# Last batch's natural scores: four row strips written in two pairs, each pair behind its own maxima, and no constant matmuls ahead of them

## The reference

```
x = layernorm(x + bitlinear_attention(x))          # block a
q = concat([ctx, x]) @ Wq                          # block b, per batch of 8
k = x @ Wk; v = x @ Wv; ssm_k = ctx @ Wsk; ssm_v = ctx @ Wsv
delta = pos[:, None] - pos[None, :]
mask = (delta >= 0) & (delta < 64)                 # for both streams
scores = einsum('bhqd,bhkd->bhqk', q, kcat) / 4 + alibi
wei = softmax(where(mask, scores, -inf)); o = wei @ vcat
x = layernorm(x + o @ Wo)
x = layernorm(x + x @ base_w.T + base_b + lora_of_top2_experts(x))   # block c
```

## Time and profile before

| | |
|---|---|
| median of 3 runs | 920.82 us (917.58, 920.82, 921.01) |
| the profiled execution | 920.37 us, of which 918.2 us are the span from first to last instruction |
| PE busy | 805.0 us (88%) |
| DVE busy | 515.8 us (56%) |
| ACT busy | 322.8 us (35%) |
| granted PE clock | 0.995 of full speed on average |

### The profile page before, as it was taken

The page is one execution under the profiler, slowest core; times in us unless marked ns, Lnnn a source line. Parts: engine busy times, 40 slices in busy tenths (PEclk is TensorE's granted clock), DMA queues, the critical chain, the costliest instruction groups (busy, mean ns, idle before and its releaser), DMA issues.

```text
span 918.2 us, 22670 instructions
## 1 busy us (share of the span) xinstructions
PE 805.0 (88%) x10223; PEld 518.4 (56%) x10275; DVE 515.8 (56%) x1061; ACT 322.8 (35%) x423; POOL 85.5 (9%) x103
## 2 busy tenths in 40 slices
PE   3888977888999989988899989988898978998996
PEld 2464763467635874467635864567545864474343
DVE  4645386437945487437845486447845383425233
ACT  5252323442243323442244323432244314230422
POOL 1102002000210012000300012000300010010001
PEclk9999999999999999999999999999999999999999
DMA  9512501000001000010001000010001000000000
GB/s 343 181 47 46 72 1 24 25 2 1 11 15 47 2 2 24 1 48 1 25 1 47 2 2 24 1 47 2 1 1 47 3 1 1 24 2 1 1 24 24
DMA packets 18879, 27.08 MB, mean 29 GB/s; under 512 B 5464, under 2 KB 7640, under 8 KB 18784
## 3 DMA queue, kind: packets, MB, share of 16 engines
q1 hardware_dynamic: 18640, 25.61, 9.3%
q10 hardware_dynamic: 144, 0.03, 0.0%
HBM read 21.44 MB, written 4.19 MB: 28 GB/s over the span
## 4 chain that ended last, share of the span: by engine, by line
PE 62%; DVE 19%; ACT 13%; issue 4%; POOL 1%; DMA 1%; ACTq 0%; POOLq 0%; SPq 0%; DVEq 0%
ACT p_b L740 9%; DVE max_b L1457 7%; PE ps L1118 7%; PE ps L1154 6%; PE ps L1039 6%; PE ps L1195 5%; PE ps L1022 4%; PE ps L1083 4%; PE ps L1059 3%; PE ps L870 2%; PE ps L943 2%; PE ps L1127 2%; PE ps L953 2%; PE ps L1047 2%; PE ps L838 2%
## 5 line engine op out<-in xcount | busy, mean ns | idle before, releaser
L740 ACT ACTIVATE p_b<-ps 128x2048 f32<-128x2048 f32 x64 | 106.5, 1664 | 116.1 <-PE ps L1127 116.1
L1457 DVE TENSOR_REDUCE max_b<-ps 128x4 f32<-128x768 f32 (+2 forms) x160 | 106.5, 709 | 39.5 <-PE ps L1097 21.3
L1083 PE MATMUL ps<-k_b,q_b 32*128 32x192 f32 (+2 forms) x1024 | 55.7, 332 | 25.7 <-DVE max_b L1457 23.6
L1118 PE MATMUL ps<-q_b,k_b 32*128 32x512 f32 (+1 forms) x512 | 66.2, 586 | 12.8 <-ACT p_b L740 7.0
L1483 DVE STREAM_TRANSPOSE o_nat<-ps 128x512 f32<-128x512 f32 x32 | 21.0, 695 | 98.2 <-PE ps L1143 98.2
L1083 PEld LDWEIGHTS ps<-k_b,q_b 32*128 32x128 f32 x1024 | 39.2, 184 | 43.1 <-DVE max_b L1457 37.1
L1143 PE MATMUL ps<-p_b,v_b 128*32 128x256 f32 (+1 forms) x1024 | 61.7, 358 | 2.0 <-ACT p_b L740 2.0
L1022 PE MATMUL ps<-c_t,wq 128*128 128x256 f32 x256 | 60.4, 385 | 2.9 <-DVE out_a L1380 1.9
L1337 DVE SCALAR_TENSOR_TENSOR nat<-ps,st_a,qkv_bias 128x512 f32<-128x512 f32 x48 | 35.3, 738 | 48.0 <-PE ps L870 47.7
L1195 PE MATMUL ps<-base_t,x_t 128*128 128x512 f32 x128 | 62.0, 609 | 0.3 <-DVE x L1562 0.3
L1039 PE MATMUL ps<-x_t,wq 128*128 128x256 f32 x256 | 60.0, 384 | 0.2 <-ACT x_t L694 0.2
(11 more groups left out here) (193 smaller groups left out, 1414.2 us busy)
## 6 DMA issues: line engine op xcount, KB each, us to landing
x_in<-x SPq DMA_DIRECT2D x8, 512.0 KB, 3.6
p_b<-ctx SPq DMA_DIRECT2D x8, 512.0 KB, 4.3
y<-x SPq DMA_DIRECT2D x7, 512.0 KB, 3.0
p_b<-L_attn_qkv_w SPq DMA_DIRECT2D x2, 1024.0 KB, 6.6
p_b<-L_xattn_Wq SPq DMA_DIRECT2D x1, 2048.0 KB, 14.8
x<-L_attn_qkv_w SPq DMA_DIRECT2D x2, 512.0 KB, 9.6
x<-L_ffn_base_w SPq DMA_DIRECT2D x2, 512.0 KB, 7.8
wo<-L_xattn_Wo SPq DMA_DIRECT2D x8, 128.0 KB, 7.5
```

Source lines behind the costliest of these rows:

```text
L740: act.activation(p_b[:, j % 2, :, 0:cols], ps[:, 4:8, 0:cols], ACT.Exp, scale=DB ** -0.5).then_inc(pb_here.sem, 1)
L1083: pe.matmul(bank(4 + r)[:, (i % 2) * N:(i % 2) * N + 2 * n * S], q_b[strip[r], i, :, :].rearrange("p h q -> p (h q)"), k_b[strip[r], half, ...
L1118: pe.matmul(bank(4 + r)[:, 0:nb * P], k_b[strip[r], half, 2 * j:2 * j + 2, :, :].rearrange("p c s k -> p (c s k)"), q_b[strip[r], 2 * j:2 ...
L1457: ins = dve.tensor_reduce(max_b[:, half, 0, i:i + k, 2 * n:2 * n + 2], ps[:, 4 + 2 * n:6 + 2 * n, :].rearrange("p r (i n) -> p i r n", i=2 ...
```

## The change

For the last batch alone (`alone`), stage b2 writes strips 0 and 1 first and then strips 2 and 3, each as a group of its own. From pair 1 on, each group waits for one count of `sb_max`: strips 0 and 1 for the maxima of banks 4 and 5 of the pair before, strips 2 and 3 for those of banks 6 and 7. The matmuls of constants ahead of the eight pairs (24 of them) are gone. Every other batch does what it did, and the lists of DVE, ACT, POOL and SP are the same.

```diff
@@ -1064,39 +1064,43 @@
             strip = [slice(r * S, (r + 1) * S) for r in range(4)]
 
             def b2(b, half, pair):
-                keep_on(b, NB - 1, (0, 0, 6, 6, 4, 4, 2, 2)[4 * half + pair])
-                if pair:
+                alone = isinstance(b, int) and b == NB - 1
+                if pair == 0:
+                    if half:
+                        mb_here(pe, b, 1)
+                    else:
+                        q_here(pe, b)
+                        k_here(pe, b)
+                        v_here(pe, b)
+                        if not alone:
+                            ct_here(pe, b + 1)
+                elif not alone:
                     sb_max(pe, b, 8 * half + 2 * pair)
-                elif half:
-                    mb_here(pe, b, 1)
-                else:
-                    q_here(pe, b)
-                    k_here(pe, b)
-                    v_here(pe, b)
-                    if not (isinstance(b, int) and b + 1 >= NB):
-                        ct_here(pe, b + 1)
                 seen = [(i, slice(max(i - 2, 0), i + 1)) for i in (2 * pair, 2 * pair + 1)]
                 o = lambda r, i, n: bank(4 + r)[:, (i % 2) * N:(i % 2) * N + 2 * n * S].rearrange("p (c k) -> p c k", c=n)
-                for i, keys in seen:
-                    n = min(i, 2) + 1
-                    for r in range(4):
-                        pe.matmul(bank(4 + r)[:, (i % 2) * N:(i % 2) * N + 2 * n * S], q_b[strip[r], i, :, :].rearrange("p h q -> p (h q)"),
-                                  k_b[strip[r], half, keys, :, :].rearrange("p c s k -> p (c s k)"),
-                                  start=(i % 2 == 0), stop=False, skip_group_check=True)
-                for i, keys in seen:
-                    n = min(i, 2) + 1
-                    for r in range(4):
-                        at = slice(r * S, r * S + 3)
-                        pe.matmul(bank(4 + r)[:, (i % 2) * N:(i % 2) * N + 2 * n * S], slopes[at, half, :], places[at, keys, :], start=False, stop=False, skip_group_check=True)
-                for i, keys in seen:
-                    n = min(i, 2) + 1
-                    for r in range(4):
-                        if i < 2:
-                            mm = pe.matmul(o(r, i, n)[:, i, :], rep[strip[r], :], mask_nat[strip[r], 1, :], start=False, stop=True, skip_group_check=True)
-                        else:
-                            mm = pe.matmul(o(r, i, n)[:, 0:3:2, :], rep[strip[r], :], mask_nat[strip[r], :, :], start=False, stop=True, skip_group_check=True)
-                        if i % 2 and r % 2:
-                            mm.then_inc(sb_full.sem, 1)
+                for strips in ((range(2), range(2, 4)) if alone else (range(4),)):
+                    if alone and pair:
+                        sb_max(pe, b, 8 * half + 2 * pair - 1 + strips[0] // 2)
+                    for i, keys in seen:
+                        n = min(i, 2) + 1
+                        for r in strips:
+                            pe.matmul(bank(4 + r)[:, (i % 2) * N:(i % 2) * N + 2 * n * S], q_b[strip[r], i, :, :].rearrange("p h q -> p (h q)"),
+                                      k_b[strip[r], half, keys, :, :].rearrange("p c s k -> p (c s k)"),
+                                      start=(i % 2 == 0), stop=False, skip_group_check=True)
+                    for i, keys in seen:
+                        n = min(i, 2) + 1
+                        for r in strips:
+                            at = slice(r * S, r * S + 3)
+                            pe.matmul(bank(4 + r)[:, (i % 2) * N:(i % 2) * N + 2 * n * S], slopes[at, half, :], places[at, keys, :], start=False, stop=False, skip_group_check=True)
+                    for i, keys in seen:
+                        n = min(i, 2) + 1
+                        for r in strips:
+                            if i < 2:
+                                mm = pe.matmul(o(r, i, n)[:, i, :], rep[strip[r], :], mask_nat[strip[r], 1, :], start=False, stop=True, skip_group_check=True)
+                            else:
+                                mm = pe.matmul(o(r, i, n)[:, 0:3:2, :], rep[strip[r], :], mask_nat[strip[r], :, :], start=False, stop=True, skip_group_check=True)
+                            if i % 2 and r % 2:
+                                mm.then_inc(sb_full.sem, 1)
 
             def b2_max(b, half):
                 keep_on(b, NB - 1, 3)
```

## The result

The changed kernel takes 926.0 us (median of 6 runs, 924.5 to 930.1) against 916.9 us for the kernel before in the same comparison (6 runs, 915.9 to 921.0). I had forecast 920.2 us and no change that can be measured. The time lies outside my range, and what happened is the rival to which I gave 0.06.

A forecast was written before the change was run, and what follows sets the result against it. Bound: PE and DVE alternating in stage b2, 3.11 us a round, falling to about 2.2. Half 0 gains 0.85 us, 0.65 remains after half 1, where PE bounds: 920.82 - 0.65 = 920.2 us, range 916.9 to 922.0.

The forecast's parts named there:

- The 24 constants: 0 us: Stage b2, last batch: removing the constant matmuls ahead of its pairs frees 0 us, since they end before the wait does.
- rival 4: Clock falls because constants no longer fill PE's waits: 941 if low all stage, 921.9 for one fall; chance 0.06.
- the under 0.4 us that I had allowed: Ahead of pair 3 of half 1, two constants touch the path, with under 0.4 us.
- A group of two strips costs what one of four does: PE in stage b2: two strips take 1.0 us first, 0.95 following another; a pair costs 1.95 where it cost 1.0.
- my 2.2: PE-DVE rounds in stage b2 fall from 3.11 to about 2.2 us wherever nothing else stands in PE's list.
- my 0.65: Half 0: pair 0's second group, 0.65 us ahead of line 1195, makes pair 1 start that much later.
- The block-c matmuls and three constants run into the turning: End of each half: line 1195 (1.82 us) and three constants (0.65) run straight into turning the maxima; PE is last wait.
- the second group: Strips 2 and 3 of a pair: 0.95 us more of PE behind the first group's 1.0.
- The drain rule: Changing tiling mode between strip and full-height matmuls drains PE: 0.21 us each instead of 0.14, making the gain 0.45.

## Why the prediction was wrong

**The step that failed** is "The 24 constants: 0 us", with the ground given against rival 4: "in the new order PE waits little, since two groups fill 1.95 of 2.2 us of a round". I took PE's busy time as what keeps the clock. It isn't. The changed kernel's clock fell behind 3.12 busy us of 3.40, and constants of the same length kept it on 64 rows and not on 32. The two rows that rival 4 weighed against each other already differed in height. The stretch at 895 us, 2.21 us busy and followed by no fall, has matmuls on all 128 rows alone; the one at 41.7 us, 2.01 us busy and followed by a fall, has mostly matmuls on 32 rows:

```profile
896.28 0.66 PE L1168 MATMUL ps<-cf,x 128*128 128x128 f32 x4 [0.90 <-ACT x L675]
...
43.63 0.45 PE L943 MATMUL ps<-q,k 32*128 32x128 f32 x8
```

The constants cost little on the path of the kernel before, as I wrote (at full clock, half 1 is 14.69 us with them and 14.31 without, the under 0.4 us that I had allowed), but they were what held the clock in two places: in the rounds of half 0, and at ACT's copy ahead of half 1. I saw the second ("some 1.1 us" without a matmul) and the question about two strips of four, named both, and gave them 0.06 together.

**The size of rival 4.** I priced a clock that stays low for the whole stage at 941 us and one fall at 1.75. In between lies what happened, 20.4 us at half clock. With the clock up, the same order takes 26.65 us (the two kernels with two constants in half 0, with and without four at the copy), so the falls cost 36.46 - 26.65 = 9.8 us, 3.2 in half 0 and 6.6 in half 1. The single fall of half 0 alone was 3.2, not 1.75, because it was twice as long as the one in the earlier trace rows.

**What held.** A group of two strips costs what one of four does: rounds of 2.25 us against my 2.2, and pair 1 started 3.26 us after pair 0 (820.08 to 823.34), where it was 2.72 before (824.56 to 827.28): 0.54 later against my 0.65. The block-c matmuls and three constants run into the turning, and PE is the last wait. At full clock the order, with two or six constants in it, gains 1.22 us of the stage, where I had 0.65. The term that was too large is the second group. In the timeline above it begins 0.77 us after the first (844.17), while the first's bias and mask still run on the other strips, and the pair is off PE's list after 1.90 us (843.40 to 845.30), the change of height included, where I counted 1.00 + 0.95 + 0.14 = 2.09. Three pairs in half 1 make most of the 0.57 us of difference.

**The drain rule** was weighed at 0.2 us, and it played no part in the result. A price for the change of height can be read from the kernel with constants on 32 rows, where there is none between the masks and the constants:

```profile
826.85 0.29 PE L1099 MATMUL ps<-cb 32*128 32x128 bf16 x8
826.96 1.45 PE L1069 MATMUL ps<-cb 32*128 32x512 bf16 x6
```

The constants start 0.11 us after the masks, and on 128 rows 0.22 us after them (831.32 to 831.54). So the change costs some 0.1 us there. But the matmul behind it still starts before the recorded end of the masks, on 128 rows there (831.54 against 831.61) as for line 1200 in the timeline above (845.30 against 845.37), so the trace shows no wait for the full end, as far as its modelled ends go.

**What stays open.** Which runs fall behind the gap and which don't (two of ten didn't, with the same program). How the loss divides between the missing constants and the groups of two strips is open too. Without constants four strips fell too, but mostly for less time, and with all constants back two strips had no fall in the profile; what each adds in a given run isn't shown. And by which measure of the work the clock is granted: the height of the matmuls counts, but no run varied their width, or the kind of number, by itself.

## What to carry to other kernels

Matmuls of constants in a wait may be almost free on the path and still be worth 10 us, because the clock hangs on them. Before they are taken out, ask of each place what full-height work is left there, and look at the granted clock after, not at PE's busy share, and in several runs, since one profile may show no fall. Splitting a pass over four strips into two passes halves how much of the array works at a time, and here took 1.90 us of PE where one pass took 1.15. For the clock, one constant of 128 rows a round, or the idle strips run along, made up for it. And where the clock falls, few constants in the right wait keep it up (four at ACT's copy took 6.6 us off half 1), and more of them on a path that PE bounds cost time (all 24: 2.4 us over before).

## What the runs showed of the hardware

- The granted clock fell to half while PE was busy for 3.12 of 3.40 us, with matmuls on two of the four strips of 32 rows. The Trainium skill (TensorE: Matmul & The Clock Gate, section Terms) calls the gate a monitor that watches how busy PE is. By this trace, busy in the sense of the profile isn't enough: stretches of the kernel before with 2.90 of 3.40 us were followed by full clock.
- Matmuls on other strips, run side by side with a group, left the rounds at 2.25 us at full clock (the kernel with filled strips, half 0: 12.31 us, against 12.23 without them and with two constants).
- A group on strips 2 and 3 begins before the one on strips 0 and 1 is through, 0.77 us after its start. The Trainium skill (the same page, Part 3: Packing small matmuls — row/col tiling) says that matmuls and weight loads overlap where their row groups differ, and the trace agrees.
- Once down behind the gap, the clock stayed at half for 13.6 us in which PE was busy throughout, with groups of two strips and the block-c matmuls, in the profile of the changed kernel.
- A fall isn't a property of the program alone. The kernel with two constants in half 0 and none at the copy had a clock of 0.999 and 915.6 to 915.8 us in two of ten runs, and 0.983 to 0.990 and 922.9 to 929.2 us in eight.
